# An order of instructions changed in a pipelined stack of six attention layers: GpSimd's root, ScalarE's normalisation, TensorE's row transposes

## The reference

```
L0: x = ln(x + mha(x, x));  x = ln(x + mha(x, ctx));  x = ln(x + relu(x W1 + b1) W2 + b2)
L1: x = x + mha(rms(x), rms(x));  x = x + mha(rms(x), ctx);
    x = x + shared(rms(x)) + sum of the 2 best of 8 experts, weighted by a softmax of their logits
L2: x = ln(x + mha(x, ctx))
L3: x = x + mha(x, ctx);  x = x + relu(x w1 + b1) w2 + b2
```

## Time and profile before

| | |
|---|---|
| median of 3 runs | 702.21 us (697.53 to 704.16) |
| profiled execution | 700.95 us, span 699.0 us, mean granted clock 0.973 |
| TensorE matmul busy | 606.7 us, 87% |
| VectorE busy | 529.2 us, 76% |
| ScalarE busy | 476.9 us, 68% |
| GpSimd busy | 415.4 us, 59% |
| chain that ended last | PE 48%, issue 21%, DVE 14%, ACT 8%, POOL 7% |
| line 494, GpSimd | 96 times, 1758 ns on average |
| line 1147, VectorE | 80 times, 212 to 820 ns, median 217 ns |

### The profile page before, as it was taken

How to read it: one execution, slowest core, us unless ns; L and a number is a source line. 1 busy time by engine, 2 the same in 40 slices (tenths; PEclk the granted TensorE clock), 3 DMA queues, 4 the chain that set the end, 5 groups by cost and what they waited for, 6 DMA issues and landing times.

```text
span 699.0 us, 24529 instructions
## 1 busy us (share of the span) xinstructions
PE 606.7 (87%) x8126; PEld 438.3 (63%) x8126; DVE 529.2 (76%) x1210; ACT 476.9 (68%) x1355; POOL 415.4 (59%) x641
## 2 busy tenths in 40 slices
PE   6888998989998989999767658899996878999996
PEld 3555656666666666666544434799994546666773
DVE  2988899777778899999999852344435788888894
ACT  3677788788878887878655534354533567788994
POOL 5676676778888765565566675055554466665220
PEclk9999999999999999999999978999999899999997
DMA  6433433222444401010111001122225000100110
GB/s 199 122 93 90 105 84 84 53 66 56 107 125 114 126 25 31 26 31 26 32 32 32 25 29 36 35 61 69 66 62 135 17 25 24 30 12 22 36 31 27
DMA packets 49817, 41.97 MB, mean 60 GB/s; under 512 B 6569, under 2 KB 44333, under 8 KB 48704
## 3 DMA queue, kind: packets, MB, share of 16 engines
q1 hardware_dynamic: 41472, 23.13, 11.9%
q10 hardware_dynamic: 5984, 13.45, 8.1%
q0 software_dynamic: 2272, 4.24, 1.8%
HBM read 25.41 MB, written 14.79 MB: 57 GB/s over the span
## 4 chain that ended last, share of the span: by engine, by line
PE 48%; issue 21%; DVE 14%; ACT 8%; POOL 7%; DMA 1%; DVEq 0%; ACTq 0%; POOLq 0%; SPq 0%
PE ps L598 6%; PE ps L824 5%; PE ps L835 5%; PE ps L631 4%; PE ps L759 3%; DVE inv L1107 3%; ACT normed L922 3%; PE ps L687 3%; PE ps L790 3%; PE ps L770 2%; PE ps L708 2%; PE ps L616 2%; DVE prob L1156 2%; PE ps L688 2%; DVE picked L1178 2%
## 5 line engine op out<-in xcount | busy, mean ns | idle before, releaser
L494 POOL TENSOR_TENSOR k_by_j<-k_t,cst 128x1024 f32<-128x1024 f32 (+1 forms) x96 | 168.8, 1758 | 102.8 <-ACT k_t L952 63.0
L1140 DVE TENSOR_REDUCE top<-ps 128x16 f32<-128x1024 f32 (+1 forms) x96 | 108.3, 1128 | 16.6 <-PE ps L598 16.4
L631 PEld LDWEIGHTS ps<-cst,prob 128*128 128x128 f32 x704 | 78.5, 143 | 57.4 <-ACT prob L986 41.1
L986 ACT ACTIVATE prob<-prob 128x1024 f32<-128x1024 f32 (+1 forms) x96 | 95.2, 992 | 20.4 <-DVE prob L1156 19.8
L1156 DVE TENSOR_TENSOR prob<-ps,top 128x1024 f32<-128x1024 f32 (+1 forms) x96 | 108.3, 1128 | 0.7
L1107 DVE RECIPROCAL inv<-ps 128x128 f32<-128x128 f32 x96 | 91.5, 953 | 22.0 <-PE ps L770 21.2
L598 PE MATMUL ps<-k_by_j,q_t 64*64 64x512 f32 (+1 forms) x768 | 102.3, 604 | 0.5 <-POOL k_by_j L494 0.4
L631 PE MATMUL ps<-cst,prob 128*128 128x128 f32 x704 | 98.4, 282 | 1.2 <-ACT prob L986 1.2
L1000 ACT ACTIVATE v<-ps 64x64 f32<-64x64 f32 x320 | 69.0, 216 | 14.2 <-PE ps L770 11.3
L915 ACT ACTIVATE prob_t<-ps 128x512 f32<-128x512 f32 (+1 forms) x96 | 53.8, 560 | 36.2 <-PE ps L631 35.5
L540 POOL DMA_INDIRECT expert_out<-rows_out,rows_in x39 | 38.3, 982 | 53.8 <-DVE rows_out L1309 27.0
(11 more groups left out here) (159 smaller groups left out, 1267.3 us busy)
## 6 DMA issues: line engine op xcount, KB each, us to landing
sorted_rows<-zero_rows ACTq DMA_DIRECT2D x32, 276.2 KB, 2.7
stage_m<-in_m SPq DMA_DIRECT2D x80, 64.0 KB
mow<-in_mow SPq DMA_DIRECT2D x18, 256.0 KB, 3.0
stage_kv<-in_ctx_t SPq DMA_DIRECT2D x64, 64.0 KB
rows_in<-sorted_rows SPq DMA_DIRECT2D x39, 65.0 KB
x_t<-in_x_t SPq DMA_DIRECT2D x16, 64.0 KB, 1.9
stage_kv<-in_x_t SPq DMA_DIRECT2D x16, 64.0 KB
stage_kv<-x_t SPq DMA_DIRECT2D x16, 64.0 KB
```

What stands on the lines that cost most here:

```text
L494: pool.tensor_tensor(k_by_j[:, p, 0:nj, :], k_t[:, p:p + 1, :].broadcast_to([128, nj, TOK]), cst[:, cj:cj + nj].unsqueeze(2).broadcast_to( ...
L631: mm = pe.transpose(ps[:, 2 * p + half, k * 128:(k + 1) * 128], prob[:, p, q * 128:(q + 1) * 128], ident)
L986: act.activation(prob[:, p, 0:w], prob[:, p, 0:w], ACT.Exp, scale=float(D // heads(pr)) ** -0.5).then_inc(exp_d, 1)
L1140: dve.tensor_reduce(top[:, p, 0:nh].rearrange("p (b h) -> p b h", b=2), sc, AX.X, ALU.max).then_inc(top_d, 1)
```

## The change

Three reorderings, no operation added or removed. On GpSimd the block of stage 4 (root 502, 505, 511) comes before the block of stage 0 (key copies 494). On ScalarE the normalisation (922) comes before the first probability copy (915). On TensorE both row transposes (662, 672) leave their place behind the v projection, come behind the q and k projections, and write to `B_HEADS` in place of `B_OUT` and `B_PROJ`; they wait for the heads of the pair in stage 4, and the product with v (759) waits for their copies out. ScalarE takes the feed-forward's x_t copy (940) behind the q and k copies.

```diff
-        FB, OUT, XT = (slice(128 * n, 128 * n + 128) for n in range(1, 4))
+        OUT, XT, FB = (slice(128 * n, 128 * n + 128) for n in range(1, 4))
...
# GpSimd, slot
-                pr = at(OFF_PROJ)
-                if pr is not None:
-                    p, nj = pr.p, heads(pr) // 2
-                    cj = C_J16 if nj == 8 else C_J8
-                    wait_pair(pool, k_e, pr)
-                    wait_pair(pool, score_d, pr, 2)
-                    pool.tensor_tensor(k_by_j[:, p, 0:nj, :], k_t[:, p:p + 1, :].broadcast_to([128, nj, TOK]),
-                                       cst[:, cj:cj + nj].unsqueeze(2).broadcast_to([128, nj, TOK]), ALU.mult)\
-                        .then_inc(kj_d, 1)
                 pr = at(OFF_OUT)
                 if pr is not None and POST[pr.phase] != "none":
...
+                pr = at(OFF_PROJ)
+                if pr is not None:
...
+                    (the same key copies)
...
# TensorE, slot
-                    turned = at(OFF_XT + 1)
-                    if turned is not None:
-                        wait_pair(pe, xt_e, turned)
                     mm = pe.matmul(ps[:, B_PROJ, 256:384], stage_kv[:, p, :], wat[:, ph, 2, :], start=True, stop=True)
                     mm.then_inc(vproj_d, 1)
-
-                done = follows(at, OFF_FB, FF)
-                if done is not None:
-                    wait_own(pe, f_xn, done)
-                    pe.transpose(ps[:, B_OUT, FB], xn_f[:, done.p, :], ident).then_inc(f_back, 1)
-                pr = at(OFF_XT)
-                if pr is not None:
-                    wait_pair(pe, norm_d, pr)
-                    projected = at(OFF_PROJ + 1)
-                    if projected is not None:
-                        wait_pair(pe, k_e, projected)
-                    valued = at(OFF_V + 1)
-                    if valued is not None:
-                        wait_pair(pe, v_e, valued)
-                    pe.transpose(ps[:, B_PROJ, XT], row_buffer(pr), ident).then_inc(xt_d, 1)
...
# behind the q and k projections
+                divided = at(OFF_OUT)
+                pr = follows(at, OFF_FB, FF)
+                if pr is not None:
+                    if divided is not None:
+                        wait_pair(pe, heads_d, divided)
+                    wait_own(pe, f_xn, pr)
+                    pe.transpose(ps[:, B_HEADS, FB], xn_f[:, pr.p, :], ident).then_inc(f_back, 1)
+                pr = at(OFF_XT)
+                if pr is not None:
+                    if divided is not None:
+                        wait_pair(pe, heads_d, divided)
+                    wait_pair(pe, norm_d, pr)
+                    pe.transpose(ps[:, B_HEADS, XT], row_buffer(pr), ident).then_inc(xt_d, 1)
...
# ahead of the product with v
                     wait_pair(pe, heads_d, pr, 1)
+                    turned = at(OFF_XT)
+                    if turned is not None:
+                        wait_pair(pe, xt_e, turned)
+                    turned = follows(at, OFF_FB, FF)
+                    if turned is not None:
+                        wait_own(pe, f_xt, turned)
                     wait_pair(pe, pt0_e, pr)
...
# ScalarE, slot: the block at(OFF_XT) with line 922 now stands ahead of the block at(OFF_PV) with line 915;
# the x_t copy of line 940 moves behind the q and k copies:
+                pr = follows(at, OFF_FB, FF)
+                if pr is not None:
+                    wait_own(act, f_back, pr)
+                    turned = at(OFF_XT)
+                    if turned is not None:
+                        wait_pair(act, xt_d, turned)
+                    act.activation(x_t[:, bass.ds(pr.i * TOK, TOK)], ps[:, B_HEADS, FB], ACT.Copy, scale=v("n1"))\
+                        .then_inc(f_xt, 1)
...
-                    dst, src = x_t[:, bass.ds(pr.i * TOK, TOK)], ps[:, B_PROJ, XT]
+                    dst, src = x_t[:, bass.ds(pr.i * TOK, TOK)], ps[:, B_HEADS, XT]
```

More of the change, by code:

```diff
@@ L513, in slot @@
                         pool.sem_inc(shift_d, 1)
+                pr = at(OFF_PROJ)
+                if pr is not None:
+                    p, nj = pr.p, heads(pr) // 2
+                    cj = C_J16 if nj == 8 else C_J8
+                    wait_pair(pool, k_e, pr)
+                    wait_pair(pool, score_d, pr, 2)
+                    pool.tensor_tensor(k_by_j[:, p, 0:nj, :], k_t[:, p:p + 1, :].broadcast_to([128, nj, TOK]),
+                                       cst[:, cj:cj + nj].unsqueeze(2).broadcast_to([128, nj, TOK]), ALU.mult)\
+                        .then_inc(kj_d, 1)
                 pr = follows(at, OFF_R2, RO)
@@ L692, in slot @@
                     wait_pair(pe, heads_d, pr)
-                    before = follows(at, OFF_FB, FF)
-                    if before is not None:
-                        wait_own(pe, f_xt, before)
                     pe.matmul(ps[:, B_OUT, OUT], heads_t[:, pr.p, :], wat[:, pr.phase, 3, :], start=True, stop=True)\
@@ L908, in slot @@
                         .then_inc(l_o, 1)
[L909 to L915, removed]
                 pr = at(OFF_XT)
@@ L923, in slot @@
                         .then_inc(norm_d, 1)
+                pr = at(OFF_PV)
+                if pr is not None:
+                    p = pr.p
+                    w = 128 * (heads(pr) // 4)
+                    wait_pair(act, pv_d, pr, 2)
+                    wait_pair(act, pt0_d, pr)
+                    act.activation(prob_t[:, p, 0, 0:w], ps[:, 2 * p, 0:w], ACT.Copy).then_inc(pt0_e, 1)
                 pr = follows(at, OFF_FB, FF)
@@ L935, in slot @@
                     act.activation(prob_t[:, p, 1, 0:w], ps[:, 2 * p + 1, 0:w], ACT.Copy).then_inc(pt1_e, 1)
[L937 to L941, removed]
                 pr = at(OFF_PROJ)
```

## The result

The changed kernel takes **695.76 us** (median of 11 runs, 692.96 to 699.85); the kernel before took 702.21 in as many (697.53 to 704.76). The ratio is 0.9917 (95% interval 0.9893 to 0.9941): 0.8% faster, where 706 was forecast.

The account below looks back on a forecast made before the run. No engine was full over the whole span, so stretches had different limits; 4.8+2.5+10.5-1.2-2.9-10.1+1.5 = +5.1 us on a profiled 700.95 gave 706, range 693 to 717.

Parts of the forecast that it names:

- I count it held through that one too: Layer-norm slots: mask conversion held through key copies and line 478 (0.46), giving 5.55 us a slot.
- the lower bound: Layer-norm slots: same sum with VectorE let in right after the key copies, 5.09 us a slot.
- Slots 8 to 22 with phase 4's eight: Layer-norm slots at 5.55 us each: +4.8 for slots 8 to 22, +2.5 for eight of phase 4.
- the port rival: VectorE gets in as soon as key copies end; layer-norm slots cost 5.09, total 696 us; chance 0.20.
- slots 36 to 42: Earlier spread, no minus and shift: 7.45 twice, 6.4 once, then three at 4.75; -1.2 us.
- phases 2 and 3: RMS-norm slots 42 to 55: squares clear of key copies, about 4.65 a slot; -2.9 us, bounds -1 and -5.
- feed-forward: Slots 22 to 36: one slot at 6.4, 13 at 8.35; +10.5 us, bounds +9.2 and +17.6.
- The loop: Feed-forward slots: `y`, spread, root, key copies, next slot's line 444, VectorE's line 1118 onward; sum 8.47, taken as 8.35.
- Routing: Slots 55 to 64: line 1178 loses most of its 2.54, GpSimd becomes the bound; -10.1 us, bounds -12 and 0.
- The rival: Routing gains nothing if the path from root through projections to `y` exceeds 7.4 us; total 716; chance 0.28.
- Phase 5: GpSimd's order unchanged; new wait for the x_t copy, 0.1 for each of 15 slots: +1.5, bounds -1 and +5.
- Edges: Phase edges counted at nothing, since VectorE's combine work and GpSimd's sums overlap either way.

Follow-up runs that it names:

- the one with two inputs: Changed kernel with VectorE's mask conversion made an operation with two SBUF inputs instead of one input and a constant; median 701.12 us, ratio 1.0027.
- the experiment: Kernel before the change, with GpSimd's two short row copies of the routing slots (lines 483, 486) made sums; median 701.19 us, ratio 1.0028.
- the rest alone: Changed kernel with GpSimd's two blocks back in the old order, leaving the row transposes and ScalarE's order; median 683.24 us, ratio 0.9771.
- keys first: Changed kernel, but GpSimd makes key copies ahead of the root in slots followed by a feed-forward root; median 671.32 us, ratio 0.9617.
- GpSimd's order alone: Kernel before the change with only GpSimd's root, minus and shift put ahead of its key copies; median 694.09 us, ratio 0.9949.
- the transpose moved to the projections' bank: Changed kernel with key copies first in feed-forward slots, plus the attention's row transpose in free columns of `B_PROJ`; median 662.88 us, ratio 0.9467.

## Why the prediction was wrong, step by step

**The step that failed: "I count it held through that one too".** The mask conversion was to be held through line 478 as well as the key copies. It was let in right behind the key copies, in this kernel and in the one with two inputs. The layer-norm slot has the length of the lower bound (5.12 against 5.09 there), and term by term: 1.07 to the end of the spread, 0.08 to the root (0.10 by my estimate), 0.93 to the key copies, 1.90 to the subtraction, 1.13 to the next `y`. Slots 8 to 22 with phase 4's eight came to -1.1 instead of +7.3. These 8.4 us are more than the forecast of +5.1, so they alone turn its sign; the port rival's 696 is the time that came, and it had 0.20. That it came so close is luck in part: it shares the other terms, and among these misses of +4.6 (slots 36 to 42), +2.1 (phases 2 and 3) and +1.2 (the end) were cancelled by -2.8 (feed-forward), -3.8 (phase 4's start) and -1.9 (the start). Its being right isn't a rule for the chip: line 1178 before and line 1196 in the experiment were passed over. I took one of two cases in my own rows as the pattern for the other; between ends that the rows bear out equally, the chances should have been even. The Trainium skill, page "SBUF — State Buffer", section "Who interferes with whom", has the order of issue decide who blocks; the conversion agrees with that (it ended 0.07 to 0.12 behind the key copies when it started ahead of GpSimd's next instruction, 0.08 behind line 478 when it didn't), the two instructions that were passed over (2.54 and 2.08 us) don't.

**Feed-forward slots: mechanism and length right.** The first two slots took 5.93 and 6.24, the twelve behind them 100.04, 8.34 each on average against 8.35 forecast. The loop began one slot later than I had it, and TensorE's freed time shortened the first two (6.08 and 6.24 with the rest alone): hence +7.7 and not +10.5. Removing the loop brought back 20.5 us there. In slots 36 to 42 the sign was wrong: from one key copy to the next they took 7.33, 7.33, 7.33, 6.49, 5.74 and 5.40, for which I had 7.45 twice, 6.4 and three times 4.75. The loop held one slot longer, and the three slots behind it didn't come down to 4.75. With keys first the six take 34.47, so 5.7 of this was the loop.

**Phases 2 and 3: right mechanism, gain lost.** The squares stand clear of the key copies (median 0.29, before 0.82):

```profile
L1239 DVE CUSTOM_DVE_ANT_0 squares<-y x32: 291/292/335, 235.6 to 408.3; 128x128 f32<-128x128 f32 x32
```

The gain was to be -2.9 with -1 as the bound if the new wait ate it. It did: -0.8. GpSimd's order alone gives -5.0, and so does the transpose moved to the projections' bank. The forecast had this cost as a bound only.

**Routing: right** (-9.9, forecast -10.1). The last five slots take 6.37 to 6.73. The rival's path isn't the 7.4 that it needed, though it comes close to GpSimd's own: the root waits up to 0.42 for the spread. GpSimd's order alone gives -8.3, the rest alone -0.6.

**Phase 5: right** (+1.7, forecast +1.5); the kernel with the transpose in the projections' bank takes 4.5 off it, so the wait costs 0.3 for each of 15 slots and the kernel without it is 2.8 below the kernel before; the prediction had 0.35 a slot of cost and 0.2 given back.

**Edges: wrong at nothing.** Phase 4's first slots gave -3.8 by the root that no longer stands behind key copies which wait for k themselves; GpSimd's order alone gives -3.5. The start gave -1.9 and the end took 1.2; the kernel with keys first has the same order up to slot 8 and took 46.30 there against 45.39, so how much of these is the change's stays open.

The range held the time; the likeliest case and its sign were wrong.

## What to carry to other kernels

Before an instruction is moved behind another on an in-order engine, list what then stands behind both in the next slot: here a gain of 2.3% by TensorE's and ScalarE's order was mostly lost because line 444 stood behind key copies, and choosing GpSimd's order by stage brought 3.8% in place of 0.8%. An instruction ahead of others is also worth moving back where it waits for something itself, not only for its length. Where rows show a hold-up going two ways, give both their chance rather than take the costlier one as the rule, and price every new wait in each stretch, since a wait that hides in one (slots of 5.1 us) costs 0.28 in each slot of the next (4.75 in place of 4.47).

## What the runs showed of the hardware

- The conversion and the squares of VectorE, whose operands are all in SBUF, are held until the end of GpSimd's key copies when they meet them: the conversion takes 0.22 alone and up to 1.09 so, the squares 0.29 and 0.82 to 1.73. Instructions that read PSUM (lines 1141 and 1157) kept their 1.22 and 1.21 beside the same key copies.
- At the end of the key copies a waiting conversion was let in ahead of, or beside, the next GpSimd instruction in 27 of 27 places, but small VectorE instructions were passed over across short GpSimd instructions that follow each other (2.54 and 2.08 us until the key copies' end). Neither two SBUF inputs in place of one nor GpSimd's copies explain it by themselves; the size of the VectorE instruction (128x16 against 128x128), its types and the length of the GpSimd instruction ahead weren't tested.
